# Sixteen gathers issued in the opening instead of between the last scatters of a graph network's edge stage

## What is computed

```python
for k in range(3):
    e = edge_vector @ edge_W[k] + edge_b[k]
    msg = relu(x[src] + e)
    agg = segment_sum(msg, dst)
    z = (1 + eps[k]) * x + agg
    h = relu(batch_norm(z @ W1[k] + b1[k]))
    x = relu(layer_norm(h @ W2[k] + b2[k]))
```

## Time and profile before

| | us |
|---|---|
| median of three runs | 1617.09 |
| the three runs | 1615.91, 1617.09, 1629.36 |
| the profiled execution's own time | 1622.57 |
| its span, first to last instruction | 1620.8 |
| mean granted PE clock of it | 0.848 of full |

### The profile page before, as it was taken

The page is one execution under the profiler, slowest core; times in us unless marked ns, Lnnn a source line. Parts: engine busy times, 40 slices in busy tenths (PEclk is TensorE's granted clock), DMA queues, the critical chain, the costliest instruction groups (busy, mean ns, idle before and its releaser), DMA issues.

```text
span 1620.8 us, 33542 instructions
## 1 busy us (share of the span) xinstructions
PE 1189.3 (73%) x12492; PEld 1001.6 (62%) x12492; DVE 924.2 (57%) x1858; ACT 548.4 (34%) x1146; POOL 858.3 (53%) x842
## 2 busy tenths in 40 slices
PE   5566665447887787787588887878856878787886
PEld 3333332236776787676478777767855767777775
DVE  8475474456666666666445455454563455565557
ACT  1232231214344444444133333333422333333333
POOL 2677677655554555451755455454255554454550
PEclk8877786777898988998688898998967899988997
DMA  8899998876665566657255555555544555555552
GB/s 221 310 329 324 321 352 293 285 241 185 206 179 157 179 177 183 178 174 242 79 173 145 160 159 165 160 146 166 169 120 129 169 147 169 163 158 157 161 155 59
DMA packets 252731, 309.89 MB, mean 191 GB/s; under 512 B 53005, under 2 KB 169791, under 8 KB 252583
## 3 DMA queue, kind: packets, MB, share of 16 engines
q1 hardware_dynamic: 208734, 218.79, 44.3%
q0 software_dynamic: 33280, 82.06, 16.2%
q10 hardware_dynamic: 10569, 6.97, 1.8%
HBM read 200.17 MB, written 107.55 MB: 190 GB/s over the span
## 4 chain that ended last, share of the span: by engine, by line
PE 62%; issue 19%; DVE 7%; another core or an unknown queue 6%; DMA 3%; ACT 1%; SPq 1%; ACTq 0%; DVEq 0%; POOL 0%
PE ps L1522 33%; PE ps L1549 10%; PE ps L1539 8%; PE ps L1503 6%; DMA ep_dram<-terms 2%; PE ps L1573 2%; DVE terms L1071 2%; PE ps L1558 1%; PE ps L1565 1%; PE ps L1571 1%; PE ps L1505 1%; DVE hot_stage L1089 1%; SPq L465 0%; DMA attr_x<-attr_dram 0%
## 5 line engine op out<-in xcount | busy, mean ns | idle before, releaser
L638 POOL DMA_INDIRECT rows<-table_dram,src_i x416 | 420.7, 1011 | 426.1 <-DVE terms L1174 244.4
L1522 PE MATMUL ps<-xs,early_words 125*128 125x128 bf16 x2720 | 295.2, 233 | 81.1 <-issue 67.5
L1167 DVE TENSOR_TENSOR terms<-ps,terms 128x512 f32<-128x512 f32 x156 | 107.8, 691 | 428.5 <-PE ps L1522 234.2
L1522 PE MATMUL ps<-xs,region 125*128 125x128 bf16 x2584 | 286.1, 234 | 74.1 <-issue 73.1
L638 POOL DMA_INDIRECT rows<-x_dram,src_i x208 | 214.5, 1031 | 181.1 <-DVE terms L1174 128.4
L1522 PEld LDWEIGHTS ps<-xs,early_words 125*128 125x128 fp8e4 x2720 | 237.2, 105 | 89.7 <-issue 76.2
L1503 PE MATMUL ps<-wf,attr_x 64*128 64x384 f32 x416 | 194.2, 619 | 124.6 <-issue 67.0
L1522 PE MATMUL ps<-xr,early_words 125*128 125x128 bf16 x1360 | 270.5, 233 | 19.3 <-issue 19.0
L655 POOL DMA_INDIRECT srt_dram<-region,pos_i x208 | 221.0, 1062 | 113.7 <-issue 60.7
L1522 PEld LDWEIGHTS ps<-xs,region 125*128 125x128 fp8e4 x2584 | 225.0, 105 | 89.6 <-issue 88.8
L1522 PE MATMUL ps<-xr,region 125*128 125x128 bf16 x1292 | 258.8, 233 | 27.3 <-issue 27.0
(11 more groups left out here) (135 smaller groups left out, 1859.2 us busy)
## 6 DMA issues: line engine op xcount, KB each, us to landing
ep_dram<-terms SPq DMA_DIRECT2D x52, 768.0 KB
terms<-srt_dram SPq DMA_DIRECT2D x156, 256.0 KB
terms<-ep_dram SPq DMA_DIRECT2D x156, 256.0 KB
early_words<-hotrow_dram SPq DMA_DIRECT2D x156, 104.0 KB
attr_x<-attr_dram SPq DMA_DIRECT2D x52, 256.0 KB
region<-kept_dram SPq DMA_DIRECT2D x13, 576.0 KB
early_words<-kept_dram SPq DMA_DIRECT2D x13, 576.0 KB
region<-kept_dram SPq DMA_DIRECT2D x13, 560.0 KB
```

The lines of the kernel that those rows point to most:

```text
L638: pool.indirect_dma_start(rows[:, q, t * FEAT:(t + 1) * FEAT], None, source, bass.IndirectOffsetOnAxis(ap=src_i[:, c:c + 1], axis=0),).the ...
L1167: nc.vector.tensor_tensor(terms[:, q, :], bank(q), terms[:, q, :], ALU.add).then_inc(s_added, 1)
L1522: ins = nc.tensor.matmul(bank(q)[:, c:c + FEAT], hot_g[v % 2][0:SLICE, h, at:at + P], x_part(part, FIRST[t] + k), start=k == 0 and part == ...
```

## The change

POOL waits for `src_i` right after its constants and issues the 16 gathers of body 0 there, ahead of its wait for the flag. The four groups of four between the scatters of bodies 9 to 12 go. In the branch for data that doesn't fit the fast plan, which isn't taken here, POOL waits until the gathers have landed. Nothing else differs: the later gathers, their waits and all other engines are as before.

```diff
+            pool.wait_ge(src_loaded, 16)
+            for q in range(BLOCK_QUADS):
+                gather(0, x, 0, q)
             pool.wait_ge(flag_ready, 1)
             general = pool.value_load(flag[0:1, 0:1])
             with pool.If(general == 0):
@@
                                 stage_s[:, q, t, :], None).then_inc(scattered[q], 16)
-                        if q == 1 and j >= BODIES - BLOCK_QUADS:
-                            gather(0, x, 0, j - (BODIES - BLOCK_QUADS))
@@
             with pool.Else():
+                for q in range(BLOCK_QUADS):
+                    pool.wait_ge(gathered[q], 16 * QUAD)
                 for l, source in enumerate([x] + tables):
```

## The result

The changed kernel takes 1597.7 us (median of eight runs, 1590.6 to 1608.2), the kernel before 1619.9 us in the eight runs beside it. The ratio is 0.9871, 95% interval 0.9843 to 0.9899, which is 20.9 us less, with 16.4 and 25.4 as ends. The profiled execution of the changed kernel took 1590.61 us, its span is 1588.7, against 1622.57 and 1620.8 before.

A forecast was written before the change was run, and what follows sets the result against it. The prediction took POOL's instruction pace to bound the last bodies. Removed gathers -17 us, opening +2.5 and loads 0 gave -14.5 us, from the median of 1617.09 to a forecast of 1603 us; range 1594 to 1618.

The forecast's parts named there:

- What is removed: Last bodies, 253 to 359 us: sixteen gathers off POOL, 20.2 us of its time, bounds 0 to 20.2, taken as 17 us.
- somewhat longer gaps: Last bodies: POOL's idle gaps, 9.2 us before, would grow somewhat without the gathers; one reason for taking 17 us, not 20.2.
- POOL's pace of 1.47 us: Scatter stage: POOL advances 1.47 us per instruction from 29 to 253 and 253 to 359 us, so it paces the last bodies.
- Backlog and slow spells belong together: Scatter stage: POOL's backlog and ACT's waits for late PE results (46.7 us) go together; less POOL work ends them sooner.
- the coincidence of three ends: Scatter stage: three long ACT waits end soon after POOL has issued all it could, at 70.53, 286.58 and 355.34 us.
- The opening: Before the first scatter: gathers slowed beside DVE leave POOL free at about 32 us, first scatter 2.5 us late; bounds 0 to 23.4.
- The one pair in the earlier trace: A scatter at 36.19 us overlaps a DVE instruction by 1.12 us and takes 1.96 us in place of 0.96.
- The loads: Opening: the gathers' 1 MB beside ACT's loads of x; up to 3 us of delay hidden, cost taken as 0, other bound 3.
- Hidden already: Last bodies: gathers only fill time in which POOL would wait for ACT; gain 0 to 3, 1617 us, chance 0.27.
- More than POOL's time comes off: Last bodies: slow spells go, 56 scatters take 82 us in place of 106; gain 24, 1595 us, chance 0.08.
- POOL isn't free: Opening: DVE holds the gathers past the first scatters, costing from 1.60 us per gather; slower, 1623.5 or 1634 us, chance 0.07.

The follow-up runs named there:

- the filler: Changed kernel plus sixteen POOL memsets of an unread buffer where the gathers stood; ratio to the kernel before 0.9979 (1244 us series), 0.9872 (1641 us series).
- SP's loads: Changed kernel plus sixteen plain loads of the gathers' bytes, issued by SP into an unread buffer; ratio to the kernel before 0.9919 (1244 us series), 0.9910 (1620 us series).
- the gathers twice: Changed kernel plus sixteen gathers of the same rows at the old places, into an unread buffer; ratio to the kernel before 1.0017 (1620 us series).

## Why the prediction was right, and where its reasons were not

The forecast was 1603 us, 14.5 us less; measured were 20.9 us less and 1597.7, inside the range. By the 1% bound it is faster, which had 0.34; the likelier class of the text, no change within 1%, did not come.

**What is removed, -17 us.** The term was too small: ACT's end came 22.7 us earlier and the last scatter 21.0, in the profiled pair. The sum of POOL's part does close: the last 56 scatters lost the gathers, 16.6 us busy and 4.9 ahead of them; POOL's idle time for ACT went from 9.2 us to 6.2; and a scatter took 1.092 us in place of 1.042, 2.8 us in all. That is 21.7 of the 21.3 us that went. The idle time did not grow, as "somewhat longer gaps" had it; that was the 3 us that I took off. DVE's waits for its stores went from 14.4 to 9.8 us.

**The reason under it, POOL's pace of 1.47 us.** This step fails. That POOL issued one instruction each 1.47 us in both stretches is true, but the filler puts 17.2 of the 20.2 us back on POOL and the kernel stays 21.0 us faster. An equal rate of an engine is no proof that it sets the rate. What would have told is ACT's wait for the ring, 7.6 us from 29 to 253 and none from 253 on in the kernel before. If POOL paces a stage, the engine that feeds it must wait for it. At 1244 us it does (111.3 us), and there, and only there, the argument by POOL's time fits the filler. So the forecast came within 6.4 us of the measured gain in part by luck: it was bounded by POOL's 20.2 us, and the runs at 1620 us don't show that it is POOL's time that the gathers cost.

**Backlog and slow spells belong together.** I took this as likelier than not. The waits fell from 46.7 us to 9.7 in the last bodies when the gathers left, but in the kernel that has the gathers behind the last scatter they stayed (33.6 us from 253 to 345, of 32.9 before). So the coincidence of three ends in the earlier trace rows did not show a cause. In the same stretch the waits come to 6.9 us beside the filler, 18.1 beside SP's loads and 24.4 with the gathers twice: they vary from one kernel to the next without an order that the gathers explain. Three cases picked from two timelines were too few to call one the cause of the other.

**The opening, +2.5 us.** Too dear; it is 0.1. POOL was free at 26.2 us, not at 32. Beside the four two-operand instructions of DVE from 6.36 to 12.14 us, gathers took 1.62, 1.12 and 1.12 us and not the sum of both. All sixteen together are 17.4 us busy, 2.3 us over 16 x 0.944, where I had 7.8. The one pair in the earlier trace rows, 1.0 us longer at 1.12 us of overlap, is the extreme and not the rule. By the Trainium skill, page SBUF — State Buffer, section "SBUF: two separate sides", the prediction's estimate was POOL free at 39.8, with all of DVE's 15.5 us counted. The trace disagrees: POOL was free at 26.2, and the gathers of 9.00 and 10.42 us began and ended while DVE's four two-operand instructions stood back to back, so these DMA-issuing instructions are not excluded for their whole length.

**The loads, 0.** Right: ACT's first copy is at 26.38 (26.28 before), DVE's `pos_i` at 29.30 (29.18).

**The rivals.** *Hidden already* is refuted for the gathers by the last scatter, 21.0 us earlier; for POOL's time alone, the filler at 1641 us speaks for it. *More than POOL's time comes off* (1595) is the nearest in its size, with 22.7 us at ACT's end, and the DMA engines did reach 0.96 from 253 to 338 us to do it. Its slow spells did go in the profiled pair (46.7 to 9.7 us); that they went because the gathers did is what the kernel with the gathers behind the last scatter speaks against. *POOL isn't free* did not come; the gathers took (26.2 - 4.3) / 16 = 1.37 us each from start to start, below the 1.60 at which it begins.

**What stays open.** Why sixteen gathers cost 21 to 24 us at 1620 us, when a filler of 17.2 us of POOL's time costs nothing and their bytes 0 to 13. A trace of the changed kernel beside the filler in one series of this kind would be needed first, to rule out that the series differ in this too. And what makes the 1620 us series slow: in those the granted clock is 0.83 to 0.86 against 0.91 to 0.93, but the span is 30% longer, and PE stands idle for 315 us that the profile gives no reason for. No run here changes that.

## What to carry to other kernels

Before an engine is called the bound because it is busy or keeps an even pace, look at whether its feeder waits for it: a ring or a semaphore with long waits carries the pace back, one without them can absorb work for nothing, as it did with 17 us of filler here, up to its depth. Count what a stage's end is worth at the first instruction of the next stage, not at the last of this one: 23 us at the last scatter were 9 us at the layer's end where the feeder ran a full ring ahead; where it didn't, 21 us at the last scatter were 23 at the end of body 0 and 25 at the layer's end. When an engine's queue is still full as the next stage begins, look at what the other engines do in the first 20 us of it, too: two kernels here lost there what they had won. And test the price of work in two parts, its engine time and its bytes, before explaining it by one of them.

## What the runs showed of the hardware

The kernel before took 1244 us in two series and 1620 to 1641 in three others, with the change's ratio 0.991 in one of the first kind and 0.987 in one of the second. What the gathers cost differs too: POOL's time in the one kind, not POOL's time alone in the other. One pair of traces from one series would have hidden this.

A gather of 128 rows costs POOL 0.94 us and 0.30 ahead of it, and in the opening, beside DVE's longest two-operand instructions, at most 1.62. Sixteen of them cost nothing measurable while POOL waits for its first indices.

In the kernel before PE stood idle for 315 us with nothing in the profile to wait for in a 1620 us series, and for 36 us in a 1244 us one. At the start of the first layer it issued one-hot matmuls of 0.27 us 0.7 to 2.1 us apart, for 16 us in one trace of a 1620 us series and for 21 us in one of the 1641 us series, both times beside a POOL that issued indirect DMAs without a pause.
